# Routed experts of a decoder layer: two weight pieces of the next slot move in front of the last down pieces on TensorE, and the splitting of the weights is dealt out anew to ScalarE, VectorE and GpSimd

## The chip, the core and the metric

The kernel runs on one core of one Trainium2 chip. Its time is the device time of one launch in microseconds (us). The kernel before takes 3370.57 us, the median of 3 runs (3363.94 to 3373.97). The profiled execution is one more launch. It spans 3371.7 us from its first to its last instruction. No separate duration of that launch is given beside its span, so the span stands for it here, 1.1 us from the median.

## The reference

One decoder layer in float32 over 4096 tokens of 512 channels: self-attention, cross-attention, then a feed-forward layer with a shared expert and 32 routed experts. Only the routed experts are touched by the change. For each token one expert is chosen, and the token is scaled by the sigmoid of its top logit:

```python
logits = x @ gate_w
topk_ids = jnp.argmax(logits, axis=-1)
scores = jax.nn.sigmoid(jnp.max(logits, axis=-1))[:, None]
xs = x * scores
order = jnp.argsort(topk_ids)
g = ragged_dot(xs[order], routed_gate_w, tokens_per_expert)   # 512 -> 1024
u = ragged_dot(xs[order], routed_up_w, tokens_per_expert)     # 512 -> 1024
d = ragged_dot(jax.nn.silu(g) * u, routed_down_w, tokens_per_expert)  # 1024 -> 512
out = x + shared_out + d[jnp.argsort(order)]
```

## The kernel before, in words

The layer runs as five stages, one behind the other: self-attention, cross-attention, shared expert, a short stage that builds routing tables, and the routed experts. In the last stage the sorted tokens are cut into slots of 128 rows. A slot belongs to one expert. The program has 64 slots in blocks of 8, and a table gives for each slot a kind: 0 (unused), 1 (the next slot has the same expert) or 2 (the next slot has the next expert). Every engine runs the same loop over the slots (`slots`) and branches on the kind, so the body stands twice in the program: I call it the plain body (kind 1) and the split body (kind 2). A block of 8 has an outer loop around it.

**Precision.** Each float32 matmul is done as three: a value is split into a high part, rounded to the TensorE's float32 format fp32r, and a low part, the rest; high x high, high x low and low x high are accumulated in PSUM (`split_matmuls`). So every expert's weights must be split before they are used. They come as 12 pieces of 128x1024 values (512 KB): pieces 0 to 3 are the gate and up columns of the first half of the hidden width, pieces 4 to 7 those of the second half, pieces 8 to 11 the down weights. A `high` is a cast of e_raw to e_wH (L1402), a `low` is the subtraction e_wL = e_raw - e_wH (L1407). There is one buffer of each piece, so a piece of the next expert can be split only when TensorE has used that piece of this expert for the last time. The split body does this: while the slot is computed, all 12 pieces of the next expert are split. SyncE loads each raw piece as soon as its low part is done.

**Who splits (before).** The highs of pieces 2 and 8 are VectorE's, the ten others ScalarE's. The lows of pieces 1, 4, 6 and 8 are GpSimd's (`pool_low`), the eight others VectorE's.

**A slot on TensorE (before).** Pieces 0 to 3 (gate and up, first half, 6 matmuls each), pieces 4 and 5, four transposes of the first half of h (`h_transpose(0)`, tile d_pT), pieces 6 and 7, four transposes of the next slot's x (d_pX), down piece 8, four transposes of the second half of h, down pieces 9, 10 and 11. Each piece raises the semaphore `used` by one when its last matmul ends.

**What stands between on the other engines.** ScalarE computes silu of the gate (d_sg, L1541) when a half's four pieces are done; VectorE multiplies it with the up product (`gate`, tile d_h, L1584); TensorE transposes d_h; ScalarE casts the transposed half to its high part (`h_high`, d_hH, L1545); VectorE subtracts to get its low part (`h_low`, d_hL, L1559); only then can the down pieces that use this half start. In the same way x goes through x_high (d_xH, L1529) and x_low (d_xL). VectorE adds the routed result to the base (d_og, L1602), and GpSimd scatters it to memory and gathers the rows of the slots to come (L1478).

Each engine executes its instructions in the order of the program. So a cast or a subtraction of a weight piece that is written in front of a silu, a gate, an h_high or an h_low delays it, whatever TensorE is waiting for. That order is written out by hand in the bodies: on ScalarE `high(0,1,2)`, silu(0), `high(3,4)`, h_high(0), `high(5,6)`, silu(1), x_high, h_high(1), `high(7..11)`; on VectorE `low(0,1,2)`, gate(0), `low(3,4)`, h_low(0), `low(5,6)`, gate(1), x_low, h_low(1), `low(7..11)`, d_og, where each call skips what another engine does. In the split body each weight operation first waits until `used` shows that TensorE is done with the piece.

ScalarE needs its function table loaded (ACT_TABLE_LOAD) when it changes between casts and silu. In the split body one load stands in front of the first cast and one in front of the first silu.

Of the kernel before, what the change touches and what calls it, by code (L numbers as in the profile page):

```python
# [12 lines left out]
KC = C // P  # L13
# [1339 lines left out]
class ExpertWeights:  # L1353
# [4 lines left out]
    def __init__(self, nc, ctx, Wg, Wu, Wd, mybir, bass):  # L1358
# [5 lines left out]
        self.pool_low = (1, 4, 6, 8)  # L1364
        self.dve_high = (2, 8)
# [45 lines left out]
def routed_experts(nc, ident, xs, base, weights, index, table, out, mybir, bass, ExitStack):  # L1411
# [13 lines left out]
    POOL_LOW, DVE_HIGH = weights.pool_low, weights.dve_high  # L1425
    DVE_LOW = tuple(n for n in range(PIECES) if n not in POOL_LOW)
    ACT_HIGH = tuple(n for n in range(PIECES) if n not in DVE_HIGH)
    wH, wL, wait_low = weights.wH, weights.wL, weights.wait_low
    with ExitStack() as ctx:
# [14 lines left out]
        def slots(eng, body):  # L1444
# [3 lines left out]
            with eng.Fori(0, table.shape[2] // BLOCK) as b:  # L1448
                with eng.If(look(0, b * BLOCK, 2) > 0):
                    with eng.Fori(0, BLOCK) as i:  # L1450
# [4 lines left out]
                        with eng.If(kind == 2):  # L1455
                            body(t, look(1, t, EXP), True)

# [10 lines left out]
        def _(pool):  # L1468
# [33 lines left out]
            def body(t, e, split):  # L1502
                for n in POOL_LOW:
                    if split:
                        pool.wait_ge(s["used"], PIECES * t + n + 1)
                        weights.low(pool, nc.gpsimd, e + 1, n)
                    if n == KC + 2:
                        pool.wait_ge(s["x_in"], 16 * t + 16)
                        pool.wait_ge(s["xt"], t + 2)
                        gather_x(t + 2, s["ix"], t + 2, s["x_in"])  # L1510
# [15 lines left out]
        def _(act):  # L1526
# [5 lines left out]
            def body(t, e, split):  # L1532
                def high(*pieces):
                    for n in pieces:
                        if split and n in ACT_HIGH:
                            act.wait_ge(s["used"], PIECES * t + n + 1)
                            weights.high(act, nc.scalar.copy, e + 1, n)

                def silu(n):
                    act.wait_ge(s["used"], PIECES * t + KC * (n + 1))  # L1540
# [5 lines left out]
                high(0, 1, 2)  # L1546
                silu(0)
                high(3, 4)
                h_high(0)
                high(5, 6)  # L1550
                silu(1)
                x_high(t + 1)
                h_high(1)
                high(7, 8, 9, 10, 11)
# [3 lines left out]
        def _(dve):  # L1558
# [11 lines left out]
            def body(t, e, split):  # L1570
                def low(*pieces):
                    for n in pieces:
                        if split:
                            if n in DVE_HIGH or n in DVE_LOW:
                                dve.wait_ge(s["used"], PIECES * t + n + 1)
                            if n in DVE_HIGH:
                                weights.high(dve, nc.vector.tensor_copy, e + 1, n)
                            if n in DVE_LOW:
                                weights.low(dve, nc.vector, e + 1, n)
# [22 lines left out]
                nc.vector.tensor_tensor(og[:, :], pD[:, :], bg[:, :], ALU.add).then_inc(s["sum"], 1)  # L1602
            slots(dve, body)

        @block.tensor
        def _(pe):
# [6 lines left out]

            def body(t, e, split):
                def gate_up(half, chunks):
                    for a in chunks:
                        n = half * KC + a
                        wait_low(pe, e, n)
                        for i, (x, w, first, last) in enumerate(((xH, wH, a == 0, False), (xH, wL, False, False), (xL, wH, False, a == KC - 1))):
                            for j, bank in enumerate((pG, pU)):  # L1620
                                m = nc.tensor.matmul(bank[half][:, :], x[:, a, :], w[:, n, j, :], start=first, stop=last)  # L1621
                        m.then_inc(s["used"], 1)

# [6 lines left out]
                def down(n):  # L1630
# [5 lines left out]
                    return m.then_inc(s["used"], 1)  # L1636
# [58 lines left out]
```

## Time and profile before

| | |
|---|---|
| median of 3 runs | 3370.57 us |
| span of the profiled execution | 3371.7 us |
| busy, share of the span: PE (TensorE matmul) | 2970.8 us, 88% |
| DVE (VectorE) | 2267.0 us, 67% |
| ACT (ScalarE) | 1607.3 us, 48% |
| POOL (GpSimd) | 1250.4 us, 37% |
| mean granted TensorE clock | 0.952 |
| span of the routed experts' slots | 2441.0 to 3358.6 us |

In a timeline the bracket at the end of a row is the engine's idle time before it and what ended it. The shares above are averages over five stages; what this change can do is read in the last stage alone.

### The profile page before, as it was taken

How to read it: one execution, taken by the hardware profiler on the slowest of the kernel's cores; microseconds unless marked ns; L12 is line 12 of the kernel's file. 1: busy time of each engine (PE TensorE's matmuls, PEld its weight loads, DVE VectorE, ACT ScalarE, POOL GpSimd, SP SyncE). 2: the span in 40 equal slices, each digit the busy share in tenths (PEclk: the TensorE clock that was granted, in tenths of full speed). 3: DMA queues.
4: the chain of work that ended last, by engine and by line, in shares of the span. 5: the costliest groups of instructions: out<-in, count | busy, mean ns of one | idle time of the engine just before them, and what ended most of it. 6: DMA issues, size and time to landing. Idle time of an engine off the chain costs nothing. (4 is left out here: it accounts for less than half of the span.)

```text
span 3371.7 us, 46176 instructions
## 1 busy us (share of the span) xinstructions
PE 2970.8 (88%) x13559; PEld 2361.0 (70%) x13561; DVE 2267.0 (67%) x2504; ACT 1607.3 (48%) x2696; POOL 1250.4 (37%) x701
## 2 busy tenths in 40 slices
PE   5788888888957999999869999999198999999997
PEld 3566666666746777777757888888176777777775
DVE  7989999999866555555443333333777775766777
ACT  3556666666645555555421111111166663655664
POOL 2455555555231111111100000000467674766776
PEclk8999999999988999999979999999599999999999
DMA  3100000000031111111031111111377774767774
GB/s 116 47 20 19 19 19 19 19 19 19 13 126 34 38 37 50 38 38 38 26 121 52 58 50 50 50 59 50 136 258 268 246 259 154 252 211 243 249 255 160
DMA packets 189383, 331.62 MB, mean 98 GB/s; under 512 B 23144, under 2 KB 41576, under 8 KB 189312
## 3 DMA queue, kind: packets, MB, share of 16 engines
q1 hardware_dynamic: 177520, 304.48, 27.0%
q0 software_dynamic: 11792, 26.25, 2.3%
q8 instruction: 39, 0.64, 0.1%
q14 instruction: 32, 0.26, 0.0%
HBM read 295.76 MB, written 46.66 MB: 102 GB/s over the span
## 5 line engine op out<-in xcount | busy, mean ns | idle before, releaser
L1407 DVE TENSOR_TENSOR e_wL<-e_raw,e_wH 128x1024 fp32r<-128x1024 f32 x248 | 458.8, 1869 | 56.6 <-ACT e_wH L1402 54.2
L321 DVE TENSOR_TENSOR a_p<-a_r 128x1024 f32<-128x1024 f32 x256 | 436.5, 1713 | 57.4 <-ACT a_r L200 57.1
L177 POOL TENSOR_TENSOR a_pL<-a_p,a_pH 128x1024 fp32r<-128x1024 f32 x96 | 254.8, 2655 | 444.5 <-DVE a_p L321 426.9
L200 ACT ACTIVATE a_r<-a_pS 128x1024 f32<-128x1024 f32 x256 | 263.0, 1027 | 324.4 <-PE a_pS L49 318.0
L1407 POOL TENSOR_TENSOR e_wL<-e_raw,e_wH 128x1024 fp32r<-128x1024 f32 x136 | 388.9, 2879 | 36.6 <-ACT e_wH L1402 23.1
L1402 ACT CAST e_wH<-e_raw 128x1024 fp32r<-128x1024 f32 x322 | 327.0, 1050 | 63.9 <-DMA e_raw<-in_L_ffn_routed_up_w 32.5
L705 POOL TENSOR_TENSOR b_S<-b_S,b_ri 128x1024 f32<-128x1024 f32 x64 | 121.5, 1899 | 558.4 <-DVE b_ri L802 558.4
L47 PE MATMUL a_pO<-a_pH,a_vH 128*128 128x512 f32 x512 | 217.4, 425 | 106.6 <-POOL a_pL L177 99.4
L326 DVE TENSOR_TENSOR a_pL<-a_p,a_pH 128x1024 fp32r<-128x1024 f32 x160 | 296.6, 1854 | 17.1 <-DVE a_p L321 0.5
L200 ACT ACTIVATE a_pH<-a_r 128x1024 fp32r<-128x1024 f32 x256 | 271.6, 1061 | 11.9
L1261 POOL MEMSET r_ones<- 128x128 bf16 x1 | 0.2, 205 | 658.6 <-POOLq L970 658.6
L47 PE MATMUL a_pS<-a_qH,a_kH 128*128 (+1 forms) x512 | 213.9, 418 | 5.3 <-DVE a_qL L285 5.2
L47 PEld LDWEIGHTS a_pO<-a_pH,a_vH 128*128 128x128 f32 x512 | 98.6, 193 | 169.9 <-POOL a_pL L177 93.1
L49 PE MATMUL a_pO<-a_pH,a_vL 128*128 128x512 f32 x512 | 208.0, 406 | 0.0
L48 PE MATMUL a_pS<-a_qL,a_kH 128*128 (+1 forms) x512 | 207.5, 405 | 0.0
L49 PE MATMUL a_pS<-a_qH,a_kL 128*128 (+1 forms) x512 | 206.4, 403 | 0.0
L48 PE MATMUL a_pO<-a_pL,a_vH 128*128 128x512 f32 x512 | 206.3, 403 | 0.0
L723 ACT ACTIVATE b_S<-b_S,b_nm 128x128 f32<-128x128 f32 x512 | 198.3, 395 | 0.1
L1621 PE MATMUL d_pG<-e_wH,d_xH 128*128 128x512 f32 x368 | 153.3, 417 | 8.3 <-issue 3.1
L47 PE MATMUL d_pD<-e_wH,d_hH 128*128 128x512 f32 x368 | 156.5, 425 | 4.4
L718 ACT ACTIVATE b_qH<-b_pQ 128x512 fp32r<-128x512 f32 x64 | 38.4, 600 | 244.7 <-PE b_pQ L49 244.7
L1621 PE MATMUL d_pU<-e_wL,d_xH 128*128 128x512 f32 x368 | 146.6, 398 | 0.0
(292 smaller groups left out, 7911.0 us busy)
## 6 DMA issues: line engine op xcount, KB each, us to landing
e_raw<-in_L_ffn_routed_gate_w SPq DMA_DIRECT2D x256, 256.0 KB, 3.6
e_raw<-in_L_ffn_routed_up_w SPq DMA_DIRECT2D x256, 256.0 KB, 4.6
e_raw<-in_L_ffn_routed_down_w SPq DMA_DIRECT2D x128, 512.0 KB
a_xg<-in_x SPq DMA_DIRECT2D x8, 1024.0 KB, 5.4
a_xb<-in_x SPq DMA_DIRECT2D x32, 256.0 KB, 2.7
x<-a_o SPq DMA_DIRECT2D x32, 256.0 KB, 2.2
b_xb<-x SPq DMA_DIRECT2D x32, 256.0 KB, 2.7
b_xr<-x SPq DMA_DIRECT2D x32, 256.0 KB, 3.2
```

Source lines behind the costliest of these rows:

```text
L47: nc.tensor.matmul(out, a[0], b[0], start=first, stop=False)
L48: nc.tensor.matmul(out, a[0], b[1], start=False, stop=False)
L49: return nc.tensor.matmul(out, a[1], b[0], start=False, stop=last)
L177: nc.gpsimd.tensor_tensor(pL[:, c % 4, :, :], p[:, c % 2, :, :], pH[:, c % 4, :, :].bitcast(F32), ALU.subtract).then_inc(s["lowP"], 1)
L200: return nc.scalar.activation(out, in_, func)
L321: nc.vector.tensor_tensor(p[:, c % 2, :, :], r[:, c % 2, :, :], r[:, c % 2, :, :], ALU.mult).then_inc(s["p"], 1)
L326: nc.vector.tensor_tensor(pL[:, c % 4, :, :], p[:, c % 2, :, :], pH[:, c % 4, :, :].bitcast(F32), ALU.subtract).then_inc(s["lowD"], 1)
L705: nc.gpsimd.tensor_tensor(S[:, j % 2, :, :], S[:, j % 2, :, :], ri[:, j % 2, :].unsqueeze(2).to_broadcast([P, SUB, KEYS]), ALU.mult).then_ ...
L723: e = nc.scalar.activation(S[:, j % 2, i, :], S[:, j % 2, i, :], ACT.Exp, bias=nm[:, j % 2, i:i + 1], accum_out=rs[:, j % 2, i:i + 1])
L1402: copy(self.wH[:, n, :, :], self.raw[:, n, :, :]).then_inc(self.high_count(n), 1)
L1407: unit.tensor_tensor(self.wL[:, n, :, :], self.raw[:, n, :, :], self.wH[:, n, :, :].bitcast(self.F32), self.sub).then_inc(self.low_count(n ...
L1621: m = nc.tensor.matmul(bank[half][:, :], x[:, a, :], w[:, n, j, :], start=first, stop=last)
```

## The change

It changes three things, all in the routed experts' stage.

1. **TensorE.** Pieces 0 and 1 of a slot (`AHEAD`) are computed in the slot before, behind the second transposes of h and in front of down pieces 10 and 11. A slot now runs: pieces 2, 3, 4, 5 and 6, `h_transpose(0)`, piece 7, x transposes, down pieces 8 and 9, `h_transpose(1)`, pieces 0 and 1 of the next slot, down pieces 10 and 11. The very first slot has its two pieces computed before the loop, and the last slot computes two that nobody uses.
2. **Who splits.** ScalarE makes all twelve highs. VectorE makes ten lows, GpSimd two: `pool_low` is (3, 7).
3. **Where the splitting stands.** On VectorE `low(0)`, gate(0), `low(1,2,4)`, h_low(0), `low(5)`, gate(1), x_low, `low(6)`, h_low(1), `low(8,9)`, d_og, `low(10,11)`. On ScalarE `high(0,1)`, silu(0), `high(2,3,4)`, h_high(0), `high(5)`, silu(1), x_high, `high(6,7)`, h_high(1), `high(8..11)`. GpSimd does its two lows, then the gather of x.

The waits on `used` are counted with `after(t, n)`. For pieces 0 and 1 it returns 12 t + 2, the count that is reached when the whole slot before, down piece 11 included, is done.

```diff
-        self.pool_low = (1, 4, 6, 8)
-        self.dve_high = (2, 8)
+        self.pool_low = (3, 7)
+        self.dve_high = ()
...
+    AHEAD = (0, 1)
+    ORDER = (2, 3, 4, 5, 6, 7, 8, 9, *AHEAD, 10, 11)
...
+        def after(t, n):
+            return PIECES * t + len(AHEAD) + (0 if n in AHEAD else ORDER.index(n) + 1)
...
@@ scalar
-                        if split and n in ACT_HIGH:
-                            act.wait_ge(s["used"], PIECES * t + n + 1)
+                        if split:
+                            act.wait_ge(s["used"], after(t, n))
                             weights.high(act, nc.scalar.copy, e + 1, n)
-                high(0, 1, 2)
+                high(0, 1)
                 silu(0)
-                high(3, 4)
+                high(2, 3, 4)
                 h_high(0)
-                high(5, 6)
+                high(5)
                 silu(1)
                 x_high(t + 1)
+                high(6, 7)
                 h_high(1)
-                high(7, 8, 9, 10, 11)
+                high(8, 9, 10, 11)
@@ vector
-                low(0, 1, 2)
+                low(0)
                 gate(0)
-                low(3, 4)
+                low(1, 2, 4)
                 h_low(0)
-                low(5, 6)
+                low(5)
                 gate(1)
                 x_low(t + 1)
+                low(6)
                 h_low(1)
-                low(7, 8, 9, 10, 11)
-                dve.wait_ge(s["used"], PIECES * (t + 1))
+                low(8, 9)
+                dve.wait_ge(s["used"], PIECES * (t + 1) + len(AHEAD))
...
+                low(10, 11)
@@ tensor
+            pe.wait_ge(s["xL"], 1)
+            pe.wait_ge(s["h"], 2)
+            gate_up(0, 0, AHEAD)
             def body(t, e, split):
-                pe.wait_ge(s["xL"], t + 1)
-                pe.wait_ge(s["h"], 2 * t + 2)
-                gate_up(0, range(KC))
-                gate_up(1, range(KC // 2))
+                gate_up(e, 0, range(KC // 2, KC))
+                gate_up(e, 1, range(KC - 1))
                 h_transpose(0)
-                gate_up(1, range(KC // 2, KC))
+                gate_up(e, 1, (KC - 1,))
                 x_transpose(s["x_in"], 16 * t + 16)
                 pe.wait_ge(s["sum"], t + 1)
                 down(GU)
+                down(GU + 1)
                 h_transpose(1)
-                for n in range(GU + 1, PIECES):
-                    down(n)
+                pe.wait_ge(s["xL"], t + 2)
+                gate_up(e + 1 if split else e, 0, AHEAD)
+                down(GU + 2)
+                down(GU + 3)
```

**The order on VectorE, between gate(0) and h_low(0) of the split body.** Here d_h is the product of gate(0), e_wL a low part of a weight piece and d_hL the low part of the transposed h. Before:

```order
L1584 TENSOR_TENSOR d_h<-d_sg,d_pU 128x512
L1575 REGISTER_ALU
L1382 REGISTER_ALU
L1407 TENSOR_TENSOR e_wL<-e_raw,e_wH 128x1024
L1559 TENSOR_TENSOR d_hL<-d_pT,d_hH 128x512
```

And after the change, with the same names:

```order
L1585 TENSOR_TENSOR d_h<-d_sg,d_pU 128x512
L1382 REGISTER_ALU
L1407 TENSOR_TENSOR e_wL<-e_raw,e_wH 128x1024
L1579 REGISTER_ALU
L1382 REGISTER_ALU
L1407 TENSOR_TENSOR e_wL<-e_raw,e_wH 128x1024
L1579 REGISTER_ALU
L1382 REGISTER_ALU
L1407 TENSOR_TENSOR e_wL<-e_raw,e_wH 128x1024
L1564 TENSOR_TENSOR d_hL<-d_pT,d_hH 128x512
```

One low part stood between the two, and now three do, those of pieces 1, 2 and 4.

**The order on TensorE, behind the second transposes of h.** d_pT are the transposes, d_pD the down product, d_pG and d_pU the gate and up products. Before:

```order
L1627 MATMUL d_pT<-ident,d_h 128x128 x4
L1385 REGISTER_ALU
L47 MATMUL d_pD<-e_wH,d_hH 128x512
L48 MATMUL d_pD<-e_wL,d_hH 128x512
L49 MATMUL d_pD<-e_wH,d_hL 128x512
```

After the change:

```order
L1633 MATMUL d_pT<-ident,d_h 128x128 x4
L1652 REGISTER_ALU
L1385 ISA
L1623 MATMUL d_pG<-e_wH,d_xH 128x512
L1623 MATMUL d_pU<-e_wH,d_xH 128x512
L1623 MATMUL d_pG<-e_wL,d_xH 128x512
L1623 MATMUL d_pU<-e_wL,d_xH 128x512
L1623 MATMUL d_pG<-e_wH,d_xL 128x512
L1623 MATMUL d_pU<-e_wH,d_xL 128x512
```

Two gate and up pieces (the second has the same six rows) stand where a down piece stood, and the down piece that needs the second half of h comes behind them. Since those two pieces left the slot's front, the first transposes of h now have one piece and the x transposes between themselves and down piece 8, where they had two pieces and the x transposes.

## Rows read from the trace of the kernel before

**Rows 1.** Windows, the stage of the slots: busy us (x) per engine, PEclk, DMA.

```profile
2441.00:3359.00 918.00, 864.54 (x3864) 670.10 (x3864) 677.30 (x586) 534.67 (x617) 626.20 (x397) 1.00 0.69 236
```

**Rows 2.** Windows, one per slot, sum rows: plain, then three kinds of split.

```profile
sum 282.28, PE 278.41 PEld 217.17 DVE 133.75 ACT 73.93 POOL 120.67; mean PE 18.56 PEld 14.48 DVE 8.92 ACT 4.93 POOL 8.04
...
sum 218.51, PE 205.94 PEld 160.02 DVE 167.06 ACT 158.09 POOL 166.25; mean PE 18.72 PEld 14.55 DVE 15.19 ACT 14.37 POOL 15.11
...
sum 199.96, PE 188.09 PEld 144.94 DVE 180.78 ACT 152.15 POOL 161.90; mean PE 18.81 PEld 14.49 DVE 18.08 ACT 15.22 POOL 16.19
...
sum 195.30, PE 171.04 PEld 131.90 DVE 180.25 ACT 136.30 POOL 166.44; mean PE 19.00 PEld 14.65 DVE 20.03 ACT 15.14 POOL 18.49
```

**Rows 3.** Groups of the slots' stage: xcount | busy, mean ns | idle before, releaser.

```profile
L1407 DVE TENSOR_TENSOR e_wL<-e_raw,e_wH 128x1024 fp32r<-128x1024 f32 x248 | 458.8, 1869 | 56.6 <-ACT e_wH L1402 54.2
...
L1402 ACT ACT_TABLE_LOAD x31 | 39.8, 1283 | 89.1 <-PE d_pU L1621 89.1
```

**Rows 4.** Timeline of PE, two slots: start us, us, operation, xcount, idle and releaser.

```profile
2837.80 0.40 PE L49 MATMUL d_pD<-e_wH,d_hL 128*128 128x512 f32 x1
2838.30 0.48 PE L47 MATMUL d_pD<-e_wH,d_hH 128*128 128x512 f32 x1
...
2850.30 0.48 PE L1621 MATMUL d_pG<-e_wH,d_xH 128*128 128x512 f32 x1
...
2853.19 0.60 PE L1610 MATMUL d_pX<-ident,d_xg 128*128 128x128 f32 x4
2853.54 0.48 PE L47 MATMUL d_pD<-e_wH,d_hH 128*128 128x512 f32 x1
```

**Rows 5.** Timeline of PE and ACT where a split slot follows a split slot.

```profile
2899.31 0.44 PE L1621 MATMUL d_pG<-e_wH,d_xH 128*128 128x512 f32 x1
...
2899.51 1.06 ACT L1402 CAST e_wH<-e_raw 128x1024 fp32r<-128x1024 f32 x1 [0.35 <-PE d_pD L49]
2901.46 1.28 ACT L1402 ACT_TABLE_LOAD   x1 [0.89 <-PE d_pU L1621]
2902.76 2.00 ACT L1402 CAST e_wH<-e_raw 128x1024 fp32r<-128x1024 f32 x2
2904.78 1.28 ACT L1541 ACT_TABLE_LOAD   x1
2906.07 0.60 ACT L1541 ACTIVATE d_sg<-d_pG 128x512 f32<-128x512 f32 x1
...
2922.59 1.28 ACT L1402 ACT_TABLE_LOAD   x1 [1.80 <-PE d_pU L1621]
```

**Rows 6.** Timeline of DVE and POOL in one split slot behind a plain one.

```profile
2845.25 1.06 POOL L1478 DMA_INDIRECT d_bg<-base,d_ib  x1 [0.79 <-POOL d_ib L1490]
...
2847.42 1.23 DVE L1407 TENSOR_TENSOR e_wL<-e_raw,e_wH 128x1024 fp32r<-128x1024 f32 x1
2848.56 0.68 DVE L1584 TENSOR_TENSOR d_h<-d_sg,d_pU 128x512 f32<-128x512 f32 x1
2849.36 2.63 DVE L1407 TENSOR_TENSOR e_wL<-e_raw,e_wH 128x1024 fp32r<-128x1024 f32 x1
...
2852.51 2.83 DVE L1407 TENSOR_TENSOR e_wL<-e_raw,e_wH 128x1024 fp32r<-128x1024 f32 x1
...
2847.44 3.46 POOL L1407 TENSOR_TENSOR e_wL<-e_raw,e_wH 128x1024 fp32r<-128x1024 f32 x1 [1.13 <-PE d_pU L1621]
...
2850.86 3.40 POOL L1407 TENSOR_TENSOR e_wL<-e_raw,e_wH 128x1024 fp32r<-128x1024 f32 x1
```

**Rows 7.** Clock around the long stall of PE: timeline row, then window rows.

```profile
3028.11 0.66 PE L1627 MATMUL d_pT<-ident,d_h 128*128 128x128 f32 x4 [3.11 <-DVE d_h L1584]
...
3030.02 0.63 PE L1621 MATMUL d_pU<-e_wH,d_xL 128*128 128x512 f32 x1
3030.44 0.63 PE L1621 MATMUL d_pG<-e_wH,d_xH 128*128 128x512 f32 x1
...
3029.40:3032.80 3.40, 3.40 (x10) 2.65 (x9) 3.12 (x2) 1.98 (x2) 3.27 (x3) 0.51 0.96 366
```

More of the change, by code:

```diff
@@ L1424, in routed_experts @@
     DN = PIECES - GU
-    POOL_LOW, DVE_HIGH = weights.pool_low, weights.dve_high
+    POOL_LOW = weights.pool_low
     DVE_LOW = tuple(n for n in range(PIECES) if n not in POOL_LOW)
-    ACT_HIGH = tuple(n for n in range(PIECES) if n not in DVE_HIGH)
+    AHEAD = (0, 1)
+    ORDER = (2, 3, 4, 5, 6, 7, 8, 9, *AHEAD, 10, 11)
     wH, wL, wait_low = weights.wH, weights.wL, weights.wait_low
@@ L1502, in body @@
             def body(t, e, split):
-                for n in POOL_LOW:
-                    if split:
-                        pool.wait_ge(s["used"], PIECES * t + n + 1)
+                if split:
+                    for n in POOL_LOW:
+                        pool.wait_ge(s["used"], after(t, n))
                         weights.low(pool, nc.gpsimd, e + 1, n)
[L1507 to L1510, printed above, removed]
+                pool.wait_ge(s["x_in"], 16 * t + 16)
+                pool.wait_ge(s["xt"], t + 2)
+                gather_x(t + 2, s["ix"], t + 2, s["x_in"])
                 pool.wait_ge(s["turn"], 16 * t + 16)
@@ L1534, in high @@
                     for n in pieces:
-                        if split and n in ACT_HIGH:
-                            act.wait_ge(s["used"], PIECES * t + n + 1)
+                        if split:
+                            act.wait_ge(s["used"], after(t, n))
                             weights.high(act, nc.scalar.copy, e + 1, n)
                 def silu(n):
-                    act.wait_ge(s["used"], PIECES * t + KC * (n + 1))
+                    act.wait_ge(s["used"], after(t, KC * (n + 1) - 1))
                     nc.scalar.activation(sg[:, n, :], pG[n][:, :], ACT.Silu).then_inc(s["silu"], 1)
@@ L1572, in low @@
                     for n in pieces:
[L1573 to L1579, printed above, removed]
+                        if split and n in DVE_LOW:
+                            dve.wait_ge(s["used"], after(t, n))
+                            weights.low(dve, nc.vector, e + 1, n)
                 def gate(n):
@@ L1612, in _, with gate_up @@
             x_transpose(s["turn"], 16)
-            def body(t, e, split):
[L1615 to L1622, printed above, removed]
+            def gate_up(e, half, chunks):
+                for a in chunks:
+                    n = half * KC + a
+                    wait_low(pe, e, n)
+                    for x, w, first, last in ((xH, wH, a == 0, False), (xH, wL, False, False), (xL, wH, False, a == KC - 1)):
+                        for j, bank in enumerate((pG, pU)):
+                            m = nc.tensor.matmul(bank[half][:, :], x[:, a, :], w[:, n, j, :], start=first, stop=last)
+                    m.then_inc(s["used"], 1)
+            pe.wait_ge(s["xL"], 1)
+            pe.wait_ge(s["h"], 2)
+            gate_up(0, 0, AHEAD)
+            def body(t, e, split):
                 def h_transpose(half):
```

2 lines of the change are left out of this document (1 added, 1 removed).

## The prediction

> **What bounds the kernel now.** I went from the page to the windows of the last stage, and from there to single slots. In the stage of the slots the TensorE clock is granted in full and TensorE is busy 864.5 of 918 us [rows 1], so no more than some 50 us can be gained there, and nothing outside it changes. Next I took a window per slot, from the first gate product of a slot to that of the next [rows 2]. There are 46 slots: 31 split ones, as one table load per split body shows [rows 3], and 15 plain ones. The first slot apart, the four sum rows are, in order: 15 plain slots, 282.3 us or 18.8 each; 11 split slots behind a plain one, 218.5 us or 19.9; 10 split slots that are the second of a run, 200.0 us or 20.0; 9 that are the third or fourth, 195.3 us or 21.7. TensorE's own work is the same in all of them, about 18.5. What the split slots have more is waiting. In the last kind VectorE is busy 20.03 of 21.7 us: there it is nearly the bound. In the others it has room (15.2 and 18.1), and what counts is when its next piece of the critical chain comes up in its queue.
>
> Why do VectorE's low parts take 1.87 us in the mean [rows 3], when one takes 1.23? The rows of one slot show it [rows 6]. A GpSimd low and a VectorE low start together at 2847.4; VectorE's takes 1.23, GpSimd's 3.46. VectorE's next one starts at 2849.36, ends at 2851.99, 1.1 after GpSimd's next one began to run at 2850.86, which itself takes 3.40. The one from 2852.51 takes 2.83 and again ends about 1.1 after GpSimd's has ended (2854.26). So the two engines' subtractions take turns: each waits until the other's is done, and a GpSimd low holds the way for about 3.40 - 1.1 = 2.3 us, say 2.4. The gate, which reads PSUM, takes 0.68 in the midst of it. Both my sum and its rivals hang on this.
>
> **The change part by part.**
>
> *TensorE's order.* Two pieces take 2853.19 - 2850.30 = 2.9 us, the x transposes 0.35 [rows 4]. The matmuls are as many as before, two pieces more for the whole program. Down piece 10 now waits for h_low(1) 0.27 us (start to start 0.50 where 0.23 is the pace, [rows 4]); with 2.9 us of gate and up work in between this wait goes. A plain slot becomes 18.2 us. With the 1.1 us that one of them pays for opening a block: 15 x 18.2 + 1.1 = 274, against 282.3 by first starts: -8. What comes late next is not in the plain slots.
>
> *The wait for gate(0).* The first transposes of h used to stand six pieces after the slot's start; now five pieces, 7.1 us. In a split slot behind a split slot ScalarE ends the old slot with the cast of piece 11, which waits for TensorE's end. That is at 2899.31, where the next slot starts. The cast starts at +0.20, the branch to the next body lets the table load begin at +2.15, the casts of pieces 0 and 1 at +3.45, the second load at +5.47, silu at +6.76, ending at +7.36 [rows 5]. The change keeps these instructions in this order (`after` makes the casts of pieces 0 and 1 wait for all of the old slot). VectorE's gate follows 0.1 later and takes 0.68 [rows 6]: +8.15. So the first transposes, ready at +7.1, start at +8.2. Behind a plain slot ScalarE has branched long before and the load starts at +0.4: everything is 1.75 earlier, gate(0) ends at +6.4, no wait.
>
> Here a rule of the Trainium skill speaks against the sum. "ScalarE: Activation LUTs", section "What ACT_TABLE_LOAD costs", puts a switch of table at about 1.28 us for the load plus about 1.38 us of drain. In this trace, which decides, a load starts 0.02 after the casts' end (2904.78 behind 2904.76) and silu 0.01 after the load [rows 5]; no drain stands there. By the rule's figures, an estimate, two switches would make the slot 2.8 us longer than mine. I go by the rows.
>
> *The wait for h_low(0), the largest term.* Between gate(0) and h_low(0) VectorE had one low part; it now has those of pieces 1, 2 and 4. GpSimd's piece 3 is cast on ScalarE between 2 and 4, so GpSimd asks for its turn before VectorE reaches piece 4. GpSimd is free for it: in [rows 6] it was through with its gather at 2846.3, some 5 us after the slot began, and piece 3 is cast about 7.5 (behind plain) or 9.4 (behind split) after the start. So four subtractions follow one another behind the gate: 3 x 1.15 + 2.4 = 5.85 us. Then h_low(0), 0.65, and 0.15 until TensorE takes it up. Down piece 8 starts at 6.4 + 6.65 = +13.1 behind a plain slot, at 8.15 + 6.65 = +14.8 behind a split one. TensorE would be ready at 7.1 + 0.35 + 1.45 + 0.35 = +9.3, or 1.1 later. It stalls 3.8 and 4.4 us.
>
> *What follows.* Down pieces 8 and 9, the transposes, pieces 0 and 1, down 10 and 11: 6 x 1.43 + 0.35 = 8.9 us. Gate(1) and x_low are behind only one more low and are covered by pieces 8 and 9 (2.9 us); h_low(1), behind low 6, which may wait for GpSimd's piece 7, is covered by pieces 0 and 1. I cost these at 0; if the cover of h_low(1) fails it is 0.5 to 1 us per split slot. The slot is 13.1 + 8.9 = 22.0, or 14.8 + 8.9 = 23.7. Starts of a chain overlap by a tenth here and there; I take 21.7 and 23.5.
>
> *Who splits.* VectorE loses two casts and two turns behind GpSimd and gains two lows. Its work falls from 20.0 to about 10 x 1.15 + 2 x 2.4 + 6 x 0.65 = 20.2 at most and 18 if half of the turns are hidden. In a 23.5 us slot it no longer bounds anything. ScalarE has 12 x 1.0 + 2 x 1.28 + 5 x 0.55 = 17.3 us. Both cost 0. GpSimd's gather of x moves to behind piece 7, near +18; it is wanted a slot later: 0. The loads on SyncE come later within longer slots: 0.
>
> *Sum without the clock.* Behind plain: 11 x 21.7 = 238.7, against 218.5: +20. Behind split: 19 x 23.5 = 446.5, and 1.1 more for each of the three that open a block (the load of [rows 5] at 2922.59 comes 1.1 later after its cast than the one at 2901.46), 449.8 against 395.3: +54.5. Plain: -8. First slot: +2, two pieces that nobody had to wait for before less what the loop's start hid. Total +69.
>
> *The clock.* The one stall of this stage that is longer than 2 us, 3.11 us at 3028.11, is followed by a stretch at 0.51, where matmuls start 0.42 apart (3030.02, 3030.44) against 0.23: 3.4 x (1 - 0.23 / 0.42) = 1.5 us lost [rows 7]. The new stalls of 3.8 and 4.4 us are longer, there are 30, and what comes behind each is on the path. At least 0, at most 30 x 1.5 = 46; I take three quarters, 35, since the only row as long as these has it. The Trainium skill, "TensorE: Matmul & The Clock Gate", Part 1, has the throttled level as the default that activity releases; the trace agrees as far as that stall goes, and by that rule it would be all 30.
>
> 3371.7 + 69 + 35 = 3475.7; the median lies 1 under the profiled execution: 3475 us.
>
> **The rivals.**
>
> *A. The stalls come, the clock stays.* 3371.7 + 69 = 3441. Against it stands the 3.11 us row; for it, that it is one row.
>
> *B. VectorE's piece 4 gets its turn ahead of GpSimd's piece 3.* Then three lows stand between, 3.45, and piece 4 waits only for its cast (8.5 and 10.3): h_low(0) ends near +10.4 and +12.2, the slots are 19.4 and 21.2. Sum: 11 x 19.4 + 19 x 21.2 + 3.3 - 218.5 - 395.3 - 8 + 2 = -0.3, so 3371. That needs GpSimd to come 1 us later than I read it. Its DMA calls lengthen when VectorE is at work, which speaks for it; its 2 to 4 us of room against.
>
> *C. Faster: the engines' sums decide, not their queues.* If ScalarE reached silu(0) so early that the three lows were over before the first transposes were done, the two stalls for h go as intended. TensorE's 18.2 is the slot behind plain, and 18.2 + 1.1 that behind a split. Sum: 11 x 18.2 + 19 x 19.3 + 3.3 - 218.5 - 395.3 - 8 + 2 = -49.6: 3322. It turns faster when h_low(0) ends before about +10.5. For it: VectorE is busy 20.03 of 21.7 us in nine slots, and the work is spread better. Against it: it needs gate(0) 4 us earlier, and the cast of piece 4 alone, at +8.5 to +10.3 on ScalarE, forbids it.
>
> *D. The order does more harm.* h_low(1) late as well: 30 x 1 more, about 3500.
>
> **How the numbers follow.** Forecast 0.58, A 0.16, D 0.06 (slower: 0.80 and a part of what lies between A and B, 0.05, so 0.85), B and what is near it 0.06, C and the better half of what lies between B and C 0.09. A measurement of this kernel can tell about 0.3%, 10 us, from no change. Slower 0.85, same 0.06, faster 0.09. The range: below, A with the stalls behind plain slots 2 us shorter, 3441 - 11 x 2 = 3419, take 3420; above, all clocks fallen and half of D, 3371.7 + 69 + 46 + 13 = 3500.
>
> **What would show it.** Down piece 8 (d_pD) waits for d_hL, 3 to 4.5 us, in all 31 split slots; in the kernel before it never waits. Between a gate and the next d_hL on VectorE stand three e_wL, the last one stretched to about 3.4 us, with GpSimd's one inside. The second transposes of h no longer wait; the first wait about 1.1 us, and only behind a split slot. Plain slots take 18.2. The clock shows 0.5 stretches of 3.4 us behind most stalls. I am wrong if the e_wL of piece 4 runs before GpSimd's piece 3 (B), if ScalarE's silu(0) ends before +5 (C), or if the split slots are under 20 us.

## The result, and the profile after

The changed kernel takes 3488.43 us (median of 4 runs, 3482.0 to 3491.18), the one before 3372.27 us beside it (4 runs, 3363.94 to 3378.57). The ratio is 1.0354, with a 95% interval of 1.0339 to 1.0369: slower by 116 us. Forecast were 3475 us, within 3420 to 3500. The profiled execution spans 3486.2 us, 114.5 more than before, and the other numbers of this section are read from it.

The page after. Section 1 has the busy times, in section 2 the clock's tenths are to be seen, and of section 5 the two groups of low parts:

```profile
PE 3010.9 (86%) x13571; PEld 2408.1 (69%) x13573; DVE 2227.4 (64%) x2504; ACT 1657.2 (48%) x2758; POOL 1031.9 (30%) x639
...
PEclk9999999999979999999799999995999999999998
...
L1407 DVE TENSOR_TENSOR e_wL<-e_raw,e_wH 128x1024 fp32r<-128x1024 f32 x310 | 464.8, 1532 | 63.9 <-ACT e_wH L1402 43.3
...
L1407 POOL TENSOR_TENSOR e_wL<-e_raw,e_wH 128x1024 fp32r<-128x1024 f32 x74 | 232.4, 3145 | 179.8 <-ACT e_wH L1402 177.5
```

VectorE makes 62 lows more than in [rows 3] and is busy 40 us less, GpSimd 218 less. Both have more room, and the kernel is slower. The row of the clock shows little, since a digit of 9 takes in all from 0.90 up. The windows do better. Here is the whole stage behind the first slot (columns: us, busy us (x instructions) of PE, PEld, DVE, ACT, POOL, then the granted clock, DMA share and GB/s):

```profile
2467.90:3473.20 1005.30, 883.34 (x3781) 701.96 (x3779) 619.18 (x572) 569.37 (x661) 400.65 (x330) 0.94 0.64 208
```

[Rows 1] had the clock at 1.00. Now it is 0.94, and PE is idle for 122 us. The same four sum rows as in [rows 2], plain, behind plain, second of a run, third and fourth:

```profile
sum 272.05, PE 272.05 PEld 220.50 DVE 87.98 ACT 74.62 POOL 57.97; mean PE 18.14 PEld 14.70 DVE 5.87 ACT 4.97 POOL 3.86
...
sum 252.96, PE 219.39 PEld 174.70 DVE 179.13 ACT 174.07 POOL 125.05; mean PE 19.94 PEld 15.88 DVE 16.28 ACT 15.82 POOL 11.37
...
sum 251.83, PE 205.26 PEld 160.66 DVE 185.25 ACT 168.70 POOL 115.62; mean PE 20.53 PEld 16.07 DVE 18.52 ACT 16.87 POOL 11.56
...
sum 228.42, PE 186.60 PEld 146.09 DVE 166.83 ACT 151.99 POOL 102.02; mean PE 20.73 PEld 16.23 DVE 18.54 ACT 16.89 POOL 11.34
```

Plain slots gain 10.2 us and have no idle time left: sum and PE are the same number. The split ones lose 34.5, 51.9 and 33.1 us and take 23.0, 25.2 and 25.4 us each. These four add up to +109.2. What lies ahead of the second slot adds 5.4.

The waits of TensorE in the stage (what waited, for what: us in total, times, longest):

```profile
PE d_pD L47 <- DVE d_hL L1564: 102.6, 31, 3.7
PE d_pT L1633 <- DVE d_h L1585: 22.4, 19, 1.9
```

The first is the new one, once for each split slot. The timeline of the slot from 2559.90, which follows a split slot, shows what it waits for. The last column of a row, in brackets, is the idle time before it. PE:

```profile
2568.12 0.66 PE L1633 MATMUL d_pT<-ident,d_h 128*128 128x128 f32 x4 [1.03 <-DVE d_h L1585]
...
2570.01 0.60 PE L1613 MATMUL d_pX<-ident,d_xg 128*128 128x128 f32 x4
2574.28 0.61 PE L47 MATMUL d_pD<-e_wH,d_hH 128*128 128x512 f32 x1 [3.68 <-DVE d_hL L1564]
2574.69 0.63 PE L48 MATMUL d_pD<-e_wL,d_hH 128*128 128x512 f32 x1
...
2577.67 0.52 PE L49 MATMUL d_pD<-e_wH,d_hL 128*128 128x512 f32 x1
2578.03 0.40 PE L47 MATMUL d_pD<-e_wH,d_hH 128*128 128x512 f32 x1
2578.27 0.39 PE L48 MATMUL d_pD<-e_wL,d_hH 128*128 128x512 f32 x1
```

ACT, DVE and POOL in the same slot:

```profile
2565.35 1.28 ACT L1545 ACT_TABLE_LOAD   x1
2566.65 0.60 ACT L1545 ACTIVATE d_sg<-d_pG 128x512 f32<-128x512 f32 x1
...
2567.37 0.69 DVE L1585 TENSOR_TENSOR d_h<-d_sg,d_pU 128x512 f32<-128x512 f32 x1 [1.73 <-ACT d_sg L1545]
2567.98 5.65 DVE L1407 TENSOR_TENSOR e_wL<-e_raw,e_wH 128x1024 fp32r<-128x1024 f32 x3
2573.55 0.68 DVE L1564 TENSOR_TENSOR d_hL<-d_pT,d_hH 128x512 fp32r<-128x512 f32 x1
...
2569.21 3.33 POOL L1407 TENSOR_TENSOR e_wL<-e_raw,e_wH 128x1024 fp32r<-128x1024 f32 x1 [4.08 <-ACT e_wH L1402]
```

Between gate(0) and h_low(0) stand three lows in one row of 5.65 us. Alone they would take 3.5. The rest is GpSimd's turn, which lies inside them. The down matmuls behind the stall start 0.41 to 0.43 us apart and return to 0.23 at 2578.03. The window on them, and the one on the stretch in the slot that follows, say why:

```profile
2574.50:2577.90 3.40, 3.40 (x9) 2.62 (x9) 3.40 (x4) 0.00 (x0) 3.40 (x2) 0.50 1.00 307
2598.40:2605.20 6.80, 6.03 (x17) 4.82 (x17) 5.17 (x6) 0.85 (x1) 5.07 (x3) 0.50 0.85 279
```

There are 31 such stretches in the 45 slots, 24 of 3.4 and 7 of 6.8 us, at least one in each of the 30 split slots and none in a plain one. Before, the same slots had one [rows 7]. In 28 of the 30 a stretch lies behind the start of down 8 or runs on into it; in the other two it is over before down 8 starts.

### The profile page after: what moved, and what is told of

It reads as the page before. It is cut to its first block and busy times, and to the rows that moved or that the text cites. A ratio compares the mean times of both kernels' runs of the same rounds, so it can differ in the third digit from the quotient of the medians.

```text
span 3486.2 us, 46201 instructions
## 1 busy us (share of the span) xinstructions
PE 3010.9 (86%) x13571; PEld 2408.1 (69%) x13573; DVE 2227.4 (64%) x2504; ACT 1657.2 (48%) x2758; POOL 1031.9 (30%) x639
## 5 line engine op out<-in xcount | busy, mean ns | idle before, releaser
L1402 ACT CAST e_wH<-e_raw 128x1024 fp32r<-128x1024 f32 x384 | 388.0, 1053 | 98.5 <-PE d_pD L49 64.6
L1407 POOL TENSOR_TENSOR e_wL<-e_raw,e_wH 128x1024 fp32r<-128x1024 f32 x74 | 232.4, 3145 | 179.8 <-ACT e_wH L1402 177.5
L47 PE MATMUL d_pD<-e_wH,d_hH 128*128 128x512 f32 x368 | 170.7, 464 | 102.6 <-DVE d_hL L1564 102.6
L1549 ACT CAST d_hH<-d_pT 128x512 fp32r<-128x512 f32 x92 | 53.9, 586 | 255.1 <-PE d_pT L1633 248.9
L47 PEld LDWEIGHTS d_pD<-e_wH,d_hH 128*128 128x128 f32 x368 | 80.8, 219 | 128.8 <-DVE d_hL L1564 110.4
L48 PE MATMUL d_pD<-e_wL,d_hH 128*128 128x512 f32 x368 | 166.0, 451 | 0.0
```

Source lines behind the costliest of these rows:

```text
L47: nc.tensor.matmul(out, a[0], b[0], start=first, stop=False)
L48: nc.tensor.matmul(out, a[0], b[1], start=False, stop=False)
L1402: copy(self.wH[:, n, :, :], self.raw[:, n, :, :]).then_inc(self.high_count(n), 1)
L1407: unit.tensor_tensor(self.wL[:, n, :, :], self.raw[:, n, :, :], self.wH[:, n, :, :].bitcast(self.F32), self.sub).then_inc(self.low_count(n ...
```

## The experiments

Nine runs. Where a single run is given, the kernel before beside it is at 3367.7 us (first four) or 3368.1 (e5 to e7). Slots are given in the order plain, behind plain, second, third and fourth; each is timed from the last down matmul to the next last one.

**e1: TensorE's order alone.** Pieces 0 and 1 are moved and the waits with them; everything else is as before (ScalarE's order and the place of GpSimd's gather go back too, which the diff shown leaves out).

Against the changed kernel:

```diff
-        self.pool_low = (3, 7)
-        self.dve_high = ()
+        self.pool_low = (1, 4, 6, 8)
+        self.dve_high = (2, 8)
...
-                low(0)
+                low(0, 1, 2)
                 gate(0)
-                low(1, 2, 4)
+                low(3, 4)
                 h_low(0)
-                low(5)
+                low(5, 6)
                 gate(1)
                 x_low(t + 1)
-                low(6)
                 h_low(1)
-                low(8, 9)
+                low(7, 8, 9, 10, 11)
```

> TensorE's new order (pieces 0 and 1 ahead, piece 7 alone between the first transposes of h and the x transposes) with the splitting of the weights, its owners and its places as in the kernel before. Theory Q (the queue in front of h_low(0) and the turns that VectorE and GpSimd take are the cost): one low stands between gate(0) and h_low(0), so no long stall. Split slots behind plain 18.2 to 18.6 us, the second of a run 20.0 to 20.6, the third 21.5 to 22.2 (VectorE's work is 20 us as before), plain 18.2; total 3372 - 11 x 1.5 - 4 + 4 = about 3355. Theory A (pieces ahead leave too little time between the transposes of h and down piece 8, whoever splits): stalls of 3 us in front of down piece 8 stay, total 3440 or more.

Measured: 3405.81 us (3397.88 to 3411.91, 4 runs) against 3367.66, ratio 1.010 (1.0078 to 1.0121). It lies between what the two theories expected, a miss for both. Slots of 18.1, 20.2, 24.9 and 21.1 us. The loss sits in six of the ten second slots, which take some 27 us, with a half-clock stretch of 6.8 us in each. VectorE and GpSimd in one of them:

```profile
2915.84 0.69 DVE L1564 TENSOR_TENSOR d_hL<-d_pT,d_hH 128x512 fp32r<-128x512 f32 x1 [0.22 <-ACT d_hH L1550]
2916.78 7.92 DVE L1407 TENSOR_TENSOR e_wL<-e_raw,e_wH 128x1024 fp32r<-128x1024 f32 x1 [0.25 <-ACT e_wH L1402]
2924.62 0.68 DVE L1589 TENSOR_TENSOR d_h<-d_sg,d_pU 128x512 f32<-128x512 f32 x1
...
2916.59 7.00 POOL L1407 TENSOR_TENSOR e_wL<-e_raw,e_wH 128x1024 fp32r<-128x1024 f32 x3
```

One low of VectorE takes 7.92 us: it doesn't come up until GpSimd has done three in a row, at full speed (2.3 each). The gate of the second half stands behind it, and TensorE waits for it:

```profile
2925.35 1.11 PE L1635 MATMUL d_pT<-ident,d_h 128*128 128x128 f32 x4 [5.70 <-DVE d_h L1589]
```

Elsewhere a low of VectorE that meets one of GpSimd's gets its turn when that one is over, as in [rows 6], and takes 3.4 us at most (one took 3.9, which had begun 0.4 us ahead of GpSimd's). e9 takes this up.

**e2: the splitting alone.** The new dealing-out with the old order on TensorE.

```diff
-            return PIECES * t + len(AHEAD) + (0 if n in AHEAD else ORDER.index(n) + 1)
+            return PIECES * t + n + 1
...
                 pe.wait_ge(s["sum"], t + 1)
                 down(GU)
-                down(GU + 1)
                 h_transpose(1)
-                pe.wait_ge(s["xL"], t + 2)
-                gate_up(e + 1 if split else e, 0, AHEAD)
-                down(GU + 2)
-                down(GU + 3)
+                for n in range(GU + 1, PIECES):
+                    down(n)
```

> The new splitting (owners and places) with TensorE's order of the kernel before. Theory Q: gate(0) ends at +6.5 (behind plain: +8.5 since the cast of piece 0 waits for TensorE's first pieces) and +8.2, then 5.9 us of subtractions, h_low(0) 0.65: down piece 8 at +13.5 to +15 where TensorE is ready at +11.9. Split slots 21.5 to 22.5 us without the clock, a stall of 2.5 to 3.5 us in front of down piece 8; plain 18.5. 30 x 2 = +60, and up to +45 for the clock: 3430 to 3475. Theory A: 3365 to 3380, since TensorE's order is what costs.

Measured: 3435.83 us. Slots of 18.6, 22.4, 22.7 and 22.6 us. Its waits on TensorE:

```profile
PE d_pD L47 <- DVE d_hL L1564: 87.1, 51, 2.2
```

The splitting alone costs 68 us: 3430 to 3475 was expected by my theory, and by the rival 3365 to 3380. Its stalls come in two parts, up to 2.2 us at down 8 and up to 1.4 at a later down piece, and within the slots the clock falls 11 times, not 31. Those 11 cost nothing: the slots behind a split one take 22.4 to 22.5 us (23.4 where a block opens) with one or without. Where the matmuls behind down 8 run at half the clock, the second stall is gone; where they don't, TensorE waits those 1.4 us.

**e3: the low of piece 4 behind h_low(0).**

```diff
-                low(1, 2, 4)
+                low(1, 2)
                 h_low(0)
-                low(5)
+                low(4, 5)
```

> The changed kernel with VectorE's low of piece 4 moved behind h_low(0); nothing else. Theory Q: h_low(0) then waits for h_high(0) on ScalarE only (behind the cast of piece 4, +8.9 behind plain and +10.7 behind split). Down piece 8 at +9.8 to +11.7 behind plain (the GpSimd low of piece 3 no longer stands in front), +11.7 to +13 behind split. Split slots 19 to 20 and 21 to 22 us, stalls under 2.5 us, so few clock drops: total 3385 to 3400. Theory N (the sum of VectorE's work is what costs): nothing changes, 3488.

Measured: 3389.61 us. Slots of 18.2, 20.1, 22.1 and 22.1 us, no half-clock stretch in any. The waits:

```profile
PE d_pT L1633 <- DVE d_h L1585: 51.0, 49, 1.1
PE d_pD L47 <- DVE d_hL L1564: 13.9, 19, 0.7
```

One line moved takes 99 us off, as expected. Two lows ahead of h_low(0) are done before GpSimd comes, and the stall for d_hL falls from 3.7 to 0.7. What is late next is gate(1), now behind that low: the second transposes wait 1.05 us in every split slot.

**e4: GpSimd's piece 3 cut short.** GpSimd subtracts 8 of the 1024 columns; the rest of piece 3's low part is left out. All lows of VectorE stay where they are.

```diff
-                        weights.low(pool, nc.gpsimd, e + 1, n)
+                        if n == 3:
...
+                            nc.gpsimd.tensor_tensor(wL[:, n, :, 0:4], weights.raw[:, n, :, 0:4], wH[:, n, :, 0:4].bitcast(F32),
+                                                    ALU.subtract).then_inc(weights.low_count(n), 1)
+                        else:
+                            weights.low(pool, nc.gpsimd, e + 1, n)
```

> The changed kernel, but GpSimd subtracts only 8 of the 1024 columns of piece 3 in the routed stage (the rest of that low part is left as it was). VectorE's program is the same. Theory Q (GpSimd's low takes a turn of 2.4 us between VectorE's): the stall in front of down piece 8 falls by 2.3 us, from 3.1 to 0.8 behind plain slots and from 3.7 to 1.4 behind split ones, the low of piece 4 takes 1.2 us, split slots 19.2 and 21.1; with hardly a clock drop left the total is 3365 to 3375, 115 to 120 us less. Theory N (only VectorE's own three lows count): 3488 as before.

Measured: 3362.52 us, 126 less than the change and some 3 less than expected. Slots of 18.1, 19.3, 21.4 and 21.3 us. VectorE in a slot behind a split one:

```profile
2566.95 3.49 DVE L1407 TENSOR_TENSOR e_wL<-e_raw,e_wH 128x1024 fp32r<-128x1024 f32 x3
```

The same three lows take 3.49 us where they took 5.65. The stall goes from 3.67 to 1.53. So 2.15 us of each stall are GpSimd's turn and nothing else, and with them go nearly all of the clock's falls (one stretch left in the slots).

**e6: piece 3's low on VectorE.** One engine, four lows, no turn.

```diff
-        self.pool_low = (3, 7)
+        self.pool_low = (7,)
...
-                low(1, 2, 4)
+                low(1, 2, 3, 4)
```

> The changed kernel with the low of piece 3 on VectorE, in its place between those of 2 and 4; GpSimd keeps piece 7 alone. Between gate(0) and h_low(0) stand four VectorE lows instead of three. Theory Q: 4 x 1.15 = 4.6 us in place of 3 x 1.15 + 2.4 = 5.85: the stall is 1.2 us shorter (1.9 and 2.5), split slots 20.3 and 22.3 without the clock, which falls less often; total 3410 to 3440. Theory N: one low more, 1.15 us longer per split slot, 3520.

Measured: 3434.5 us, within the 3410 to 3440 expected; the rival's 3520 fell. Slots of 18.1, 21.3, 23.9 and 23.8 us. VectorE, a slot behind a split one:

```profile
2556.34 4.63 DVE L1407 TENSOR_TENSOR e_wL<-e_raw,e_wH 128x1024 fp32r<-128x1024 f32 x4
```

Four lows alone take 4.63 us, 1.02 less than three with a turn of GpSimd's, and the stall is 2.65 instead of 3.67. GpSimd's help with this piece costs more than the piece.

**e5: the stall filled.** Twelve matmuls, whose result is thrown away, run on TensorE while it would wait. The waits of every other engine stay.

```diff
                 pe.wait_ge(s["sum"], t + 1)
+                if split:
+                    wait_low(pe, e, PIECES - 1)
+                    for _ in range(12):
+                        nc.tensor.matmul(pD[:, :], wH[:, PIECES - 1, 0, 0:P], wH[:, PIECES - 1, 1, :], start=True, stop=True)
                 down(GU)
```

> The changed kernel with 12 matmuls of no use (128x512, into d_pD, whose content the down product then overwrites) in front of down piece 8 in every split slot: 2.8 us of TensorE work inside the stall of 3.1 or 3.7 us. Theory C (each long stall costs 1.5 us more through the clock): the granted clock stays at 1.00 in the stage, split slots take 21.5 and 23.4 us, total 3488 - 30 x 1.5 = 3440 to 3450, although TensorE does 380 matmuls more. Against C: 3488 or more.

Measured: 3435.22 us, 53 less than without the twelve, and 5 below what the clock theory expected. PE in a slot that starts at 2527.09:

```profile
2537.56 3.00 PE L1652 MATMUL d_pD<-e_wH 128*128 128x512 f32 x12
2541.53 0.50 PE L47 MATMUL d_pD<-e_wH,d_hH 128*128 128x512 f32 x1 [0.97 <-DVE d_hL L1564]
2541.87 0.39 PE L48 MATMUL d_pD<-e_wL,d_hH 128*128 128x512 f32 x1
```

The first down matmul starts 14.44 us into the slot, as in the changed kernel (14.38), so d_hL is just as late. But the pace behind it is 0.23 at once. Its window:

```profile
2541.50:2544.90 3.40, 3.37 (x17) 2.78 (x18) 3.40 (x4) 0.07 (x1) 3.25 (x2) 1.00 0.89 234
```

Seventeen matmuls in 3.4 us where the changed kernel had nine. The slots are 18.1, 21.5, 23.6 and 23.5 us, with one half-clock stretch left in them. Of the 53 us, 49 are in the slots and 4 ahead of the second one. This is the cleanest separation in the study: the order's cost (the stall) stays, the clock's cost goes.

**e7: silu(0) ahead of the first casts.**

```diff
-                high(0, 1)
                 silu(0)
-                high(2, 3, 4)
+                high(0, 1, 2, 3, 4)
```

> The changed kernel with silu(0) in front of the casts of pieces 0 and 1 on ScalarE: one table load per split slot and not two, and silu(0) 3.3 us earlier. Theory Q: VectorE still has the low of piece 0 in front of gate(0), and three lows and GpSimd's piece 3 in front of h_low(0), and these now wait for the casts. The first transposes' wait of 1.0 us goes, the stall at down piece 8 stays: 21.8 and 22.2 us per split slot without the clock, with it 23.2 and 23.7; total 3455 to 3475. If ScalarE's late silu were the cause: 3390 or less.

Measured: 3451.65 us, 3 below the expected range. Slots of 18.1, 23.3, 23.3 and 23.2 us:

```profile
PE d_pD L47 <- DVE d_hL L1563: 105.5, 31, 3.7
PE d_pT L1632 <- DVE d_h L1584: 1.6, 3, 0.5
```

The wait for the first transposes goes (19 waits before, three small ones now), and down 8 starts 13.0 us into a slot behind a split one, near the 12.6 of one behind a plain one. The stall itself stays at 3.2 to 3.5 us. An earlier gate alone doesn't help, as long as the three lows and the turn stand behind it. Four of its split slots have no half-clock stretch behind a stall of 3.5 us and take 21.9 us; those of the same kinds with one of 3.4 us take 23.5 (block openings apart). That is the clock's price once more, 1.5 us.

**e8: the chain first, everywhere.** With the causes known, silu and the gate go first in the slot, each cast and low stands behind the step of the chain that it used to delay, and GpSimd's first piece is cast only behind h_high(0).

```diff
-        self.pool_low = (3, 7)
+        self.pool_low = (3, 6)
@@ scalar
-                high(0, 1)
                 silu(0)
-                high(2, 3, 4)
+                high(0, 1, 2)
                 h_high(0)
-                high(5)
+                high(3)
                 silu(1)
                 x_high(t + 1)
-                high(6, 7)
+                high(4, 5, 6)
                 h_high(1)
-                high(8, 9, 10, 11)
+                high(7, 8, 9, 10, 11)
@@ vector
-                low(0)
                 gate(0)
-                low(1, 2, 4)
+                low(0, 1, 2)
                 h_low(0)
-                low(5)
                 gate(1)
                 x_low(t + 1)
-                low(6)
+                low(4, 5)
                 h_low(1)
-                low(8, 9)
+                low(7, 8, 9)
```

> TensorE's order of the change, with the places chosen after the chain: ScalarE silu(0), casts 0 to 2, h_high(0), cast 3, silu(1), x_high, casts 4 to 6, h_high(1), casts 7 to 11; VectorE gate(0), lows 0 to 2, h_low(0), gate(1), x_low, lows 4 and 5, h_low(1), lows 7 to 9, d_og, lows 10 and 11; GpSimd pieces 3 and 6. Theory Q: no wait of TensorE is left but the loop's own; all slots 18.2 to 18.8 us, total 3372 - 11 x 1.6 - 10 x 1.6 - 9 x 3.3 - 5 = 3303 to 3320, faster than both. Rival (the engines' sums bound the slot: ScalarE 16 us and VectorE 18 us plus waits): split slots 20 us in a run, 3340 to 3360.

Measured: 3293.18 us (3288.59 to 3295.16, 5 runs) against 3368.06 (9 runs), ratio 0.9766 (0.9743 to 0.979): faster than both kernels, and 10 us below what was expected. Of the 30 split slots 26 take 18.1 to 18.2 us, one 18.3, and the three that open a block 18.9. Two slots, each the second of a run:

```profile
3153.32:3171.46 18.14, 18.14 (x85) 14.54 (x83) 17.25 (x17) 15.50 (x18) 11.53 (x9) 1.00 1.03 370
3207.90:3226.03 18.13, 18.13 (x85) 14.72 (x84) 17.23 (x17) 15.51 (x18) 11.54 (x9) 1.00 1.01 365
```

TensorE is busy all of the slot, at a clock of 1.00. The view of the waits has no row for it in the whole stage. VectorE and GpSimd in the first of the two:

```profile
3157.52 0.68 DVE L1584 TENSOR_TENSOR d_h<-d_sg,d_pU 128x512 f32<-128x512 f32 x1
3158.25 3.50 DVE L1407 TENSOR_TENSOR e_wL<-e_raw,e_wH 128x1024 fp32r<-128x1024 f32 x3
3161.66 0.68 DVE L1563 TENSOR_TENSOR d_hL<-d_pT,d_hH 128x512 fp32r<-128x512 f32 x1
...
3162.60 2.41 POOL L1407 TENSOR_TENSOR e_wL<-e_raw,e_wH 128x1024 fp32r<-128x1024 f32 x1 [2.20 <-ACT e_wH L1402]
```

Here too three lows stand between the gate and h_low(0). But the gate is over at +4.9 us, GpSimd comes only when they are done, and h_low(0) ends at +9.0, before TensorE wants it. The later lows still meet GpSimd's and take up to 2.8 us; nothing waits for them.

**e9: a gap between GpSimd's lows.** e1 again, with GpSimd's small copy of the row indices (d_iw, some 1.2 us here) moved between its lows of pieces 1 and 4. e1's theory was that a back-to-back series of GpSimd's lows keeps VectorE out.

```diff
                         weights.low(pool, nc.gpsimd, e + 1, n)
+                    if n == 1:
+                        pool.wait_ge(s["turn"], 16 * t + 16)
+                        nc.gpsimd.tensor_copy(iw[:, :], index[:, bass.ds(t, 1)]).then_inc(s["iw"], 1)
...
-                pool.wait_ge(s["turn"], 16 * t + 16)
-                nc.gpsimd.tensor_copy(iw[:, :], index[:, bass.ds(t, 1)]).then_inc(s["iw"], 1)
```

> TensorE's new order alone, as in the run that missed (3406 us), with one thing moved: GpSimd's copy of d_iw stands between its lows of pieces 1 and 4 instead of behind that of piece 8, so that the three lows of pieces 1, 4 and 6 no longer follow one another without a gap. In the run that missed, six of the split slots behind a split slot hold a VectorE low of 7.9 us that began 0.2 us after GpSimd's first low and ended only after its third, and TensorE then waits 5.7 us. Theory T (a VectorE low that has lost its turn is let in only when GpSimd pauses): with the gap no VectorE low is longer than 3.7 us, the 5.7 us waits go, and 6 x (27.3 - 21.1) = 37 us with them: 3365 to 3372. Theory R (the 7.9 us come from something else, such as the memory or a late cast): they stay, about 3400.

Measured: 3378.67 us (10 runs) against 3367.53 (13 runs), ratio 1.003 (1.0019 to 1.0041): 27 us less than e1, but 7 above the expected range. VectorE and GpSimd in the slot that answers to the one shown of e1:

```profile
2909.74 3.33 DVE L1407 TENSOR_TENSOR e_wL<-e_raw,e_wH 128x1024 fp32r<-128x1024 f32 x1 [0.26 <-ACT e_wH L1402]
...
2909.56 2.42 POOL L1407 TENSOR_TENSOR e_wL<-e_raw,e_wH 128x1024 fp32r<-128x1024 f32 x1
2911.90 1.21 POOL L1514 COPY d_iw<-index 128x1 int32 x1
```

VectorE's low starts 0.18 us behind GpSimd's, as in e1 (0.19), and ends 1.1 us after GpSimd's first one. Eight lows of e9 start 0.18 to 0.19 behind such a first one, and all take 3.3 us; seven of e1 start 0.19 to 0.21 behind, and six of them take 7.9. All lows of 7.9 us are gone, and the waits of 5.7 us with them. The starts are nearly the same but barely overlap, so that it is the gap and not the start that saves the turn is likely, not shown. One low of e9 still takes 4.05 us, more than the 3.7 that theory T allowed; it had begun 0.5 us ahead of GpSimd's. With the gap the second slots take 21.1 us and the third and fourth 22.0, against 20.0 and 21.8 before. So TensorE's new order alone, with this mended, is still not faster: ScalarE's silu(0) chain comes 1.0 us late for transposes that stand one piece earlier (two waits of 1.1 us in a second slot), which eats what the plain slots gain.

## Why the prediction was right

**What bounds the kernel.** Right. The time is in the split slots' waits, not in any engine's sum: VectorE and GpSimd do 258 us less between them, and the kernel lost 116.

**Plain slots.** Forecast 18.2 us and -8 in all; measured 18.14 and -10.2. The 1.1 us that I kept for opening a block no longer shows in them, since the pieces that start a block are already computed.

**The wait for gate(0).** Forecast: gate(0) over at +6.4 behind a plain and +8.15 behind a split slot. Measured +6.3 and +8.16 (2567.37 + 0.69 - 2559.90), with a wait of 1.03 us only in the second kind, as forecast. The table loads had no drain behind them: silu starts 1.30 us after the second load's start, as in [rows 5]. The 1.38 us of drain per switch that the Trainium skill gives ("ScalarE: Activation LUTs", "What ACT_TABLE_LOAD costs") didn't show here.

**The three lows and GpSimd's turn.** The largest term, and right in its mechanism. Forecast 5.85 us from gate to h_low, measured 5.5; of that the turn is 2.15 us (e4), where I had put 2.4. Down 8 started at +12.5 and +14.4 (forecast 13.1 and 14.8), and TensorE was ready for it 0.2 to 0.3 us later than I had it, so the stalls were 3.06 and 3.68 us (forecast 3.8 and 4.4), and 2.2 to 2.5 in the three split slots that open a block, where a half-clock stretch lay over the work ahead of it. What follows down 8 was forecast as 8.9 us; e5, at full clock, has 8.95 and 8.96.

**The sum without the clock.** e5 measures it: 236.7 us behind plain slots against 238.7 forecast, 447.7 behind split slots against 449.8. With the plain slots, and against [rows 2], it is +60 in the stage (18.2 + 52.4 - 10.2), where my terms say +66.5. Two small slips stand in the prediction beside it: half of rival D's 30 x 1 us is 15 and not 13, which makes the upper end of the range 3502 and not 3500, and D itself comes to 3505. Rival B, piece 4 ahead of GpSimd's piece 3, fell with the rows above, and so did D: TensorE never waits for h_low(1). Rival C, faster, was to decide where h_low(0) ends before +10.5; it ended at +12.5 and +14.3. e8 shows that the point was well put: there it ends at +9.0, and the kernel is 2.3% faster than before.

**The clock: the step that was mis-sized.** I had 35 us, three quarters of 30 x 1.5. Measured: 49 inside the slots (1005.3 - 956.5); the whole runs differ by 53 (3488.4 - 3435.2), of which 4 lie ahead of the second slot. Even the 49 exceed the bound of 46 that I had set. Two things were off. Of the 30 split slots 28 paid for the clock, not three of four. The other two take 24.3 us, no longer than slots of e5 in the same place without a stretch; their only one came at +10.1, behind a wait of 1.95 us for gate(0), and was over before down 8 started. The rule of the Trainium skill, "TensorE: Matmul & The Clock Gate", Part 1, that the throttled level is the default which activity releases, pointed to all 30. The trace is nearer to that than to three quarters, but e7 has four stalls of 3.5 us without a stretch. And seven stretches were twice as long (6.8 us) and made their slots some 26 us instead of 24.9. The price behind a 3.4 us stretch was 1.5 us, as forecast (24.9 - 23.4, and 23.0 - 21.5). Rival A, stalls without a clock cost, is what e5 builds on purpose.

**The rest.** What lies ahead of the second slot: +5.4 us against +2. In the eight other kernels with this order on TensorE it ends between 2457.7 and 2465.7 us (2462.5 before, 2467.9 after), so most of it may be scatter, which no run here can divide. In all: without the clock +69 forecast and +66 measured (60 + 5.4), the clock +35 and +49. The time came out 0.4% above the forecast, and the clock is why.

**What the parts did.** The splitting alone costs 68 us (e2). TensorE's order alone costs 38 (e1), of which 27 go with the lost turns and the clock behind them, which the full change doesn't have, since its two GpSimd pieces stand apart, and 11 remain (e9). What the order adds on top of the new splitting is 53 us, and nearly all of it is clock: with the stall filled (e5) the order costs nothing on top (3435.2 us against e2's 3435.8; the 45 slots add up to 956.5 and 954.8), and the 49 in the slots that e5 takes back are what the change had more. The order makes one stall of 3.1 to 3.7 us, since h_low(0) is wanted earlier in the slot and isn't made earlier, where e2 has one of up to 2.2 and one of up to 1.4. Behind the one stall a half-clock stretch is paid for; in e2 it only takes the place of the second wait.

## What to carry to other kernels

Before giving work to a helper engine, ask what stands behind it in the queue and whether the two engines' operations exclude each other: a low on GpSimd cost the critical chain 2.15 us, on VectorE itself 1.1. A stall of 3 us on TensorE cost half as much again in clock here, so ask of each new one whether it can be broken up or filled. The half clock cost nothing where TensorE would have waited again soon anyway (e2). And when pieces are moved forward on one engine, the chain on the other engines must be moved forward by the same amount: e8 did both and won 75 us, while the move on TensorE without it lost 11 (e9) to 116 us.

## What the runs showed of the hardware

- Subtractions of two SBUF operands on VectorE and GpSimd exclude each other, instruction by instruction. VectorE's takes 1.20 to 1.23 us alone and up to 3.4 with one turn lost (in one case each of e1 and e9 3.9 and 4.1), GpSimd's 2.33 alone and up to 3.5. That was known from [rows 6]. New is that a turn can be lost three times over (7.92 us, e1), if GpSimd's come back to back and VectorE's starts 0.19 to 0.21 us behind the first. With a start 0.09 to 0.11 behind, none of the four in e1 that met such a series was lost, nor were two that started 0.34 and 0.50 behind, and with a gap of 1.1 us behind the first none of e9's was. Why 0.2 us matters is open.
- Half-clock stretches in the slots came as 3.4 or 6.8 us. Over the slots of all eleven traces, none of the 346 waits of TensorE from 0.15 to 1.6 us had one that began during the wait or up to 1.5 us behind it, 36 of 78 between 1.7 and 2.3 us did, 17 of 20 between 2.4 and 2.7 us, and 60 of 64 of 2.9 us and more. Of two equal stalls the one in which the stretch begins early gets the long one: all 15 of 6.8 us began at least 0.6 us before the wait was over, and none of the 98 of 3.4 us more than 0.57 before. What sets where it begins, nothing here shows.
- Twelve useless matmuls in a stall that is paid anyway made the kernel 53 us faster, 49 of them in the slots (e5).
- A half-clock stretch of 3.4 us cost 1.5 us where the work behind it was on the path (23.5 against 21.9 us in e7), and nothing where a wait of 1.4 us would have followed (22.4 to 22.5 us with and without in e2).
